# Edge softmax of a four-layer graph network: scans, differences and copies given to other rounds of the logits stage

## What is computed

```
h  = relu(layernorm(x))
Xq = h @ W_lin.T ;  Xv = h @ W_val.T
e  = sum_d a * leaky_relu(Xq[src] + Xq[dst]) + log(adj[src, dst] + 1e-8)    # logits, per edge and head
m  = segment_max(e, src) ; ex = exp(e - m[src])
attn = ex / segment_sum(ex, src)[src]
x += segment_sum(attn * Xv[dst], src) @ W_out.T
```

## The kernel before

| set | add, forward | backward | LESS | EXPS | TURN | TAKE | total |
|---|---|---|---|---|---|---|---|
| k = 0 | 11 | 12 | 13 | 14 | 15 | 16 | 29 |
| k = 1 | 19 | 20 | 21 | 22 | 23 | 24 | 33 |
| k = 2 | 27 | 28 | 29 | 30 | 31 | 32 | 41 |
| k = 3 | 35 | 36 | 37 | 38 | 39 | 40 | 49 |

## Time and profile before

### The profile page before, as it was taken

How to read it: one execution, slowest core, us unless ns; L and a number is a source line. 1 busy time by engine, 2 the same in 40 slices (tenths; PEclk the granted TensorE clock), 3 DMA queues, 4 the chain that set the end, 5 groups by cost and what they waited for, 6 DMA issues and landing times.

```text
span 1184.9 us, 23287 instructions
## 1 busy us (share of the span) xinstructions
PE 1155.7 (98%) x7564; PEld 1008.1 (85%) x7564; DVE 992.8 (84%) x2799; ACT 813.3 (69%) x1826; POOL 388.5 (33%) x710
## 2 busy tenths in 40 slices
PE   6999999999999999999999999999999999999998
PEld 5798898998988989989888788877777898889997
DVE  6998988888889888898888999988877789977664
ACT  4776886868868768588686766767777777753332
POOL 3130100100001001010011777766666477733332
PEclk9999999999999999999999999999999999999999
DMA  8220000000000000000000000000000000002222
GB/s 234 83 72 1 1 2 0 0 0 0 0 0 0 0 0 0 0 0 0 1 2 1 1 2 2 1 1 1 1 1 1 1 2 1 2 10 63 72 72 72
DMA packets 26319, 20.80 MB, mean 18 GB/s; under 512 B 1792, under 2 KB 22272, under 8 KB 26240
## 3 DMA queue, kind: packets, MB, share of 16 engines
q1 hardware_dynamic: 25664, 19.62, 5.8%
q10 hardware_dynamic: 576, 0.20, 0.1%
HBM read 11.42 MB, written 8.39 MB: 17 GB/s over the span
## 4 chain that ended last, share of the span: by engine, by line
PE 87%; DVE 8%; ACT 2%; issue 2%; DMA 1%; SPq 0%; DVEq 0%; ACTq 0%
PE ps L600 12%; PE ps L598 12%; PE ps L599 11%; PE ps L896 5%; PE ps L1507 5%; PE ps L1103 4%; PE ps L1515 2%; PE ps L660 2%; PE ps L646 2%; PE ps L912 2%; PE ps L882 2%; PE ps L666 2%; PE ps L672 2%; PE ps L1457 2%; PE ps L1092 2%; PE ps L1093 2%
## 5 line engine op out<-in xcount | busy, mean ns | idle before, releaser
L573 ACT ACTIVATE gate<-ps,b_lstm 128x256 f32<-128x256 f32 (+2 forms) x624 | 310.6, 565 | 96.4 <-PE ps L600 94.1
L598 PE MATMUL ps<-H_hi,w_hi 128*128 128x256 f32 (+2 forms) x624 | 210.5, 339 | 3.1 <-DVE srt L463 1.4
L599 PE MATMUL ps<-H_hi,w_lo 128*128 128x256 f32 (+2 forms) x624 | 205.1, 330 | 0.0
L600 PE MATMUL ps<-H_lo,w_hi 128*128 128x256 f32 (+2 forms) x624 | 192.6, 330 | 0.1
L131 POOL TENSOR_SCALAR rstd<-mv 128x8 f32<-128x8 f32 x16 | 5.2, 323 | 488.5 <-DVE mv L111 488.5
L598 PEld LDWEIGHTS ps<-H_hi,w_hi 128*128 128x128 f32 x624 | 117.4, 188 | 17.6 <-issue 4.0
L599 PEld LDWEIGHTS ps<-H_hi,w_lo 128*128 128x128 f32 x624 | 117.7, 189 | 8.1
L600 PEld LDWEIGHTS ps<-H_lo,w_hi 128*128 128x128 f32 x624 | 115.4, 189 | 10.5 <-DVE H_lo L527 2.0
L598 PE MATMUL ps<-hid_hi,w_hi 128*128 128x256 f32 (+2 forms) x384 | 120.3, 320 | 0.2
L599 PE MATMUL ps<-hid_hi,w_lo 128*128 128x256 f32 (+2 forms) x384 | 116.8, 311 | 0.0
L600 PE MATMUL ps<-hid_lo,w_hi 128*128 128x256 f32 (+2 forms) x384 | 106.3, 317 | 1.6 <-DVE hid_lo L527 1.0
(11 more groups left out here) (203 smaller groups left out, 3064.4 us busy)
## 6 DMA issues: line engine op xcount, KB each, us to landing
out<-x SPq DMA_DIRECT2D x32, 256.0 KB, 2.3
x<-in_x_in SPq DMA_DIRECT2D x4, 256.0 KB, 6.7
x<-in_WihT SPq DMA_DIRECT2D x1, 768.0 KB, 4.5
x<-in_WhhT SPq DMA_DIRECT2D x1, 768.0 KB, 6.7
x<-in_WihT SPq DMA_DIRECT2D x1, 256.0 KB, 8.1
x<-in_WqkvT SPq DMA_DIRECT2D x1, 192.0 KB, 4.1
w_sb<-in_W SPq DMA_DIRECT2D x1, 192.0 KB, 3.5
w_g<-in_Wg ACTq DMA_DIRECT2D x2, 64.0 KB, 4.1
```

Of the source, the lines that this page charges most:

```text
L573: nc.scalar.activation(gate[:, g, z, 0:w * GB], gate_bank(g, k, m)[:, 0:w * GB], ACT.Tanh if z == G else ACT.Sigmoid, bias=b_lstm[:, 4 * ( ...
L598: nc.tensor.matmul(dst, w_hi[:, src, p - 1, z], v_hi, start=start, stop=False)
L599: return nc.tensor.matmul(dst, w_lo[:, src, p - 1, z], v_hi, start=False, stop=False)
L600: return nc.tensor.matmul(dst, w_hi[:, src, p - 1, z], v_lo, start=False, stop=stop)
```

## The change

Only the due times change, and the waits that follow from them. The add stays in round 8 + 8k + 3 as a step of its own; both scans move to + 6, LESS to + 10, EXPS to + 11, TURN to + 12, TAKE to + 14. The first total moves from round 29 to 25. The sets then stand like this:

| set | add | both scans | LESS | EXPS | TURN | TAKE | total |
|---|---|---|---|---|---|---|---|
| k = 0 | 11 | 14 | 18 | 19 | 20 | 22 | 25 |
| k = 1 | 19 | 22 | 26 | 27 | 28 | 30 | 33 |
| k = 2 | 27 | 30 | 34 | 35 | 36 | 38 | 41 |
| k = 3 | 35 | 38 | 42 | 43 | 44 | 46 | 49 |

```diff
--- before.py
+++ after.py
@@ -1156,8 +1156,8 @@
 
 
         BURST = 4
-        FORWARD, BACKWARD, LESS, EXPS, TURN, TAKE = range(3, 9)
-        TOTAL_AT = [NG - 3] + [NG + 1 + k * PER for k in range(BH - 1)]
+        ADD_LOG, FORWARD, BACKWARD, LESS, EXPS, TURN, TAKE = 3, 6, 6, 10, 11, 12, 14
+        TOTAL_AT = [NG - 7] + [NG + 1 + k * PER for k in range(BH - 1)]
 
         def due(n, what):
 
@@ -1215,11 +1215,13 @@
 
             def softmax(n):
 
-                k = due(n, FORWARD)
+                k = due(n, ADD_LOG)
                 if k is not None:
                     dve.wait_ge(SE["d_lgp"], k * PER + PER)
                     dve.wait_ge(SE["d_near"], 4 + EC)
                     nc.vector.tensor_tensor(lgs, logit_rows, log_bc, ALU.add).then_inc(SE["e_lg"], 1)
+                k = due(n, FORWARD)
+                if k is not None:
                     dve.wait_ge(SE["e_lg"], k + 1)
                     nc.vector.tensor_tensor_scan(fwd, cut_f[:], lgs, 0.0, ALU.add, ALU.max).then_inc(
                         SE["e_fb"], 1)
@@ -1416,18 +1418,14 @@
                     pe.wait_ge(SE["e_exp"], k + 1)
                     if k == 0:
                         pe.wait_ge(SE["d_near"], 4 + EC)
-                    elif k == 1:
-                        pe.wait_ge(SE["e_ex"], EC)
                     else:
-                        pe.wait_ge(SE["e_inv"], k - 1)
+                        pe.wait_ge(SE["e_inv"], k)
                     for c in range(EC):
                         ins = nc.tensor.transpose(ps[:, 7, group_of(c)], expT[:, group_of(c)], ident[:])
                     ins.then_inc(SE["e_exTp"], 1)
                 if n in TOTAL_AT:
                     k = TOTAL_AT.index(n)
-                    pe.wait_ge(SE["e_ex"], min(k + 2, BH) * EC)
-                    if k == BH - 1:
-                        pe.wait_ge(SE["e_inv"], k)
+                    pe.wait_ge(SE["e_ex"], (k + 1) * EC)
                     for c in range(EC):
                         for j in range(EC):
                             ins = nc.tensor.matmul(ps[:, 7, E + c * P:E + (c + 1) * P], same[:, j, group_of(c)],
```

## The result

| | before | after |
|---|---|---|
| median of 10 runs each | 1185.47 us | 1188.68 us |
| lowest and highest | 1184.27 and 1186.91 | 1187.66 and 1192.02 |
| the profiled execution: time, span | 1186.77, 1184.9 | 1187.66, 1185.8 |
| P(11), the query product of round 11 | at 973.05 | at 969.32 |
| P(11) to P(31), the last query product | 79.19 | 77.67 |

The changed kernel is **slower**: ratio 1.0030, 95% interval 1.0021 to 1.0039, which is 3.2 us between the medians. By the median that is 0.27%, a little over the 0.2% that the prediction called the least that can be told from no change. The prediction had 0.9 more and a range up to 1187.7; the median lies above it.

What follows compares the result with a forecast made beforehand. The prediction took PE's rounds, held up in places by DVE's, as the bound. A first-loop gain of 1.6 us against a second-loop loss of 2.5 gave +0.9 on 1185.27: 1186.2 us, range 1183.7 to 1187.7.

Steps and rivals of the forecast that it cites:

- First loop: Rounds 11 to 31: excess over plain rounds falls from 5.6 to 4.0 us, a gain of 1.6.
- formula for P(n+1): PE's next round starts at the later of its last start + 3.18 (burst 5.24) and DVE's round start + 2.45.
- The load in round 19: ACT's table load, now in a plain round, makes the relu late; 1.50 us lost by PE's round 21.
- The rival that doubles it: Round 19: ACT stands still once more after the load, +1.28 us, net +2.2, 1187.5; chance 0.09.
- The bursts give cover: Burst rounds such as 14 and 22: both scans, 1.27 us, hide in DVE's idle stretch of 1.50.
- The slower rival: Bursts 14 and 22 give no cover, scans come back as 2 x 1.27: +3.4 us, 1188.7; chance 0.08.
- LESS ahead of the reciprocal, rounds 34 and 42: Second loop: LESS queues before the reciprocal pair on DVE with nothing to hide it, 1.08 us lost in each round.
- the pair's 2.13: DVE's reciprocal and multiply for a total, taken as 2.13 us together, in rounds 26, 34 and 42.
- 36 and 38: Second loop: set 2's turn costs PE 0.2 us in 36; scans and copies in 38 cost 0.1.
- The sum: Both loops: 2.5 us lost in the second less 1.6 gained in the first, net +0.9.
- The likeliest case: Whole kernel: the forecast of 1186.2 us, +0.9, chance 0.60, its own range 1184.8 to 1187.0.
- the slower rivals that it priced: Doubled load in round 19 (1187.5 us, chance 0.09) and bursts without cover (1188.7 us, chance 0.08).

Runs made afterwards that it cites:

- early load: Changed kernel plus one single-column exponential on ACT in burst round 10, so the table load stands there: 1189.69 us, ratio 1.0032 to before.
- the run without the lock: Changed kernel with the reciprocal written back to PSUM and the multiply reading it there: 1185.08 us, ratio 0.9999 to before.
- the first experiment: Changed kernel with the reciprocal kept in PSUM, so the multiply has one SBUF input: 1185.08 us, ratio 0.9999 to before.

## Why the prediction was wrong

By its own steps:
- **First loop.** Right, term by term: 1.5 gained to P(31) and 1.66 to the first aggregation, predicted 1.6. Rounds 20 (4.61, predicted 4.7), 25 (4.12, 4.1), 27 (3.78, 3.91), 28 (3.43, 3.43) and 29 (3.29, 3.30) are as it carries them forward. The formula for P(n+1) held.
- **The load in round 19.** Right: 19 and 20 take 7.79, 1.43 over two plain rounds, predicted 1.50. The two runs that take it away gain 1.2, since the turn, hidden under it, then shows with 0.26. The rival that doubles it falls.
- **The bursts give cover.** Right: round 15 took 3.18 with both scans in 14, and DVE had 0.20 of idle left before its leaky sum. The slower rival falls, though the result has its sign and even its number (1188.7): that agreement is chance.
- **LESS ahead of the reciprocal, rounds 34 and 42.** The step that failed: "Now LESS stands ahead of it ... Nothing is left to hide it: 1.08 lost." The queue of 1.08 is right in size, shown by the runs without the multiply's wait (5.00), though some 0.3 of it is LESS's own meeting with POOL, read from a row as it stood (0.71, where it takes 0.39 alone). But the pair's 2.13 was read from a row and set 1.09 us later as it stood, and there it takes 3.17, since its multiply meets POOL's subtraction. The runs showed intervals of 6.02 in place of the 5.0 predicted, 2.1 us in the two rounds. The rows to see it by were in the trace of before: the multiply started at 1075.56 and POOL's next subtraction at 1076.56, 1.00 later, and the multiply was about to be moved by 1.09.
- **The clock.** No term of the sum: a longer wait of PE was priced at its own length. Behind four of the six waits of 2.2 us in three profiles (after, early load, before with LESS in 34 and 42) PE ran at half clock, 1.6 us each; behind the six waits of 1.2 to 1.7 us in three others never. The profile before had a sign of it: the half-clock stretch at 792 us stands behind a wait of 1.95 us, in the attention layer.
- **36 and 38.** 0.2 and 0.1 predicted; the five intervals from aggregation 4 to 9 sum to 18.46 before and 18.71 after; round 44's turn adds 0.21 to 12-13 (3.92 in the run without the lock, 3.71 before). 0.46 in place of 0.3.
- **The sum.** 0.9 + 2.1 + 1.6 (one stretch in this profile) = 4.6, and the rounds show 4.65. The medians differ by 3.2. The rest lies ahead of P(11), where the profiles differ by up to 4.2 us, and in how many stretches each run has (the kernel before has one in its profile, at 792 us); how many the median run after has beyond the median run before isn't shown.

The likeliest case had the right sign and a mechanism that is there; what it lacked is two sizes. It gave "slower" 0.12: the slower rivals that it priced were others, and no row of POOL was laid beside the moved step.

## What to carry to other kernels

Before a step is moved within an engine's queue, lay the other engines' instructions of the new place beside it: here 1.09 us of delay became 2.13, since the multiply came under a POOL instruction with SBUF operands. Two engines that never wait for each other by a semaphore can still do so by a port; an operand in PSUM, or one round's distance, takes it away. A wait of the bounding engine can cost more than its length, so one long wait can be worse than two short ones of the same sum, and a burst's round is good cover only where there is a burst.

## What the runs showed of the hardware

- A tensor-tensor instruction on DVE of 128x256 f32 with both inputs in SBUF took 0.42 us alone and 1.46 when it began 0.08 us after a POOL tensor-tensor of 1.26 us; it ended 0.28 after POOL's. With one input in PSUM it took 0.42 at the same place, and 0.78 when POOL's was cut in two. Another of the same shape took 0.39 alone and 0.71 when it began 0.84 after POOL's.
- It can go the other way. In round 18 of the first experiment LESS began 0.13 after the record of a POOL instruction (L1187) and took its 0.39, while POOL's took 0.77, where the three like it before took 0.45.
- PE's granted clock fell to half behind some of its waits of 2.2 us, and behind none of those of 1.7 or less in the second loop. A stretch cost 1.6 us. Which wait is followed by one differs between two kernels with the same second loop (after: not in 34, in 42; early load: in 34, not in 42). In the attention layer a wait of 1.94 or 1.95 us, before L912, was followed by half clock in six of the ten profiles. By what this is decided isn't shown.
- ACT goes on right after a table load: load at 1002.29 for 1.28, exponential at 1003.59.
